# Scan inputs: log(1+e) on one vector engine at full width, magnitudes from the accumulator bank, delta ahead of C

## The reference, cut to what matters

```
xn = _rmsnorm(x, norm_w)
xz = xn @ W_in.T
xm, z = jnp.split(xz, 2, axis=-1)
...  (depthwise convolution over time, 4 taps)
xc = jax.nn.silu(xc + conv_b[None, :, None])
u = jnp.swapaxes(xc, 1, 2)
x_dbl = u @ W_x.T
dt, Bm, Cm = jnp.split(x_dbl, [DT_RANK, DT_RANK + D_STATE], axis=-1)
delta = jax.nn.softplus(dt @ W_dt.T + b_dt)
A = -jnp.exp(A_log)
y = _selective_scan(u, delta, A, Bm, Cm, Dp)
y = y * jax.nn.silu(z)
```

## Time and profile before

| | us |
|---|---|
| median of 3 runs | 3047.18 (3044.08 to 3047.55) |
| the profiled execution | 3044.58 |
| span of its trace | 3042.8 |
| TensorE busy | 2370.3 (78%) |
| VectorE busy | 1997.0 (66%) |
| ScalarE busy | 1772.5 (58%) |
| GpSimd busy | 1398.9 (46%) |
| block of `scan_inputs`, first sequence | 67.9 to 166.8 |
| block of `scan_inputs`, second sequence | 825.9 to 922.8 |

### The profile page before, as it was taken

How to read it: one execution, slowest core, us unless ns; L and a number is a source line. 1 busy time by engine, 2 the same in 40 slices (tenths; PEclk the granted TensorE clock), 3 DMA queues, 4 the chain that set the end, 5 groups by cost and what they waited for, 6 DMA issues and landing times. The chain is left out here.

```text
span 3042.8 us, 38732 instructions
## 1 busy us (share of the span) xinstructions
PE 2370.3 (78%) x12420; PEld 1202.1 (40%) x12421; DVE 1997.0 (66%) x1798; ACT 1772.5 (58%) x2733; POOL 1398.9 (46%) x540
## 2 busy tenths in 40 slices
PE   4678888888857888888886758797787499869668
PEld 1244444444324444444435123223222355545323
DVE  5689999999658999999965666515913222133440
ACT  3689999999478999999941430171064111122230
POOL 1489998999557999899941110000000300020000
PEclk7889999999988999999996878798889699979889
DMA  2130001000123000100000300010012300010000
GB/s 75 54 106 28 24 28 39 28 28 28 40 72 87 28 28 28 39 28 24 28 20 2 112 35 1 6 42 11 1 33 100 157 21 21 23 39 9 28 0 28
DMA packets 59819, 116.17 MB, mean 38 GB/s; under 512 B 13620, under 2 KB 21812, under 8 KB 58305
## 3 DMA queue, kind: packets, MB, share of 16 engines
q1 hardware_dynamic: 51104, 103.72, 10.6%
q0 software_dynamic: 8608, 11.05, 1.2%
HBM read 86.92 MB, written 27.53 MB: 38 GB/s over the span
## 5 line engine op out<-in xcount | busy, mean ns | idle before, releaser
L825 POOL TENSOR_TENSOR hs<-hs,c_bc 128x2048 f32<-128x2048 f32 x256 | 1166.2, 4556 | 67.0 <-DVE hs L876 49.3
L876 DVE TENSOR_TENSOR_SCAN hs<-decays,carry,ps 128x512 f32<-128x512 f32 x512 | 621.7, 1270 | 9.1 <-PE ps L903 8.4
L876 DVE TENSOR_TENSOR_SCAN hs<-decays,ps 128x512 f32<-128x512 f32 x512 | 610.9, 1215 | 21.0 <-PE ps L903 8.3
L911 PE MATMUL ps<-hs,sel 128*64 128x512 f32 x2048 | 498.4, 608 | 15.5 <-POOL hs L825 15.2
L839 ACT ACTIVATE decays<-delta_near,A 128x512 f32<-128x512 f32 x512 | 363.4, 723 | 23.2 <-DVEq L853 22.7
L903 PE MATMUL ps<-ident,dbu_even 128*128 128x128 f32 x2048 | 295.1, 283 | 91.9 <-DVE hs L876 63.2
L903 PE MATMUL ps<-ident,dbu_odd 128*128 128x128 f32 x2048 | 293.3, 282 | 92.3 <-DVE hs L876 60.6
L839 ACT ACTIVATE decays<-delta_far,A 128x512 f32<-128x512 f32 x512 | 358.8, 714 | 11.0 <-DVE hs L876 10.9
L847 ACT ACTIVATE dbu_odd<-du_turned,b_turned 128x512 f32<-128x512 f32 x512 | 360.8, 718 | 0.0
L847 ACT ACTIVATE dbu_even<-du_turned,b_turned 128x512 f32<-128x512 f32 x496 | 349.8, 718 | 0.0
L903 PEld LDWEIGHTS ps<-ident,dbu_even 128*128 128x128 f32 x2048 | 220.0, 141 | 241.9 <-DVE hs L876 192.5
(11 more groups left out here) (265 smaller groups left out, 2759.1 us busy)
## 6 DMA issues: line engine op xcount, KB each, us to landing
c_bc<-c_rows SPq DMA_DIRECT2D x256, 128.0 KB, 2.8
o_rows<-osb SPq DMA_DIRECT2D x32, 256.0 KB
u_rows<-u SPq DMA_DIRECT2D x4, 1024.0 KB, 8.8
d_rows<-delta SPq DMA_DIRECT2D x4, 1024.0 KB, 4.2
delta_near<-d_rows SPq DMA_DIRECT2D x4, 1024.0 KB, 9.6
hs<-u_rows SPq DMA_DIRECT2D x4, 1024.0 KB, 6.6
delta_far<-d_rows SPq DMA_DIRECT2D x4, 1024.0 KB, 12.1
w_down<-in_expert_proj SPq DMA_DIRECT2D x1, 4096.0 KB, 36.5
```

The source lines that it names most:

```text
L825: pool.tensor_tensor(x, x, spread(c_bc[:, g, :], 4), ALU.mult).then_inc(weighed.sem, 1)
L876: dve.tensor_tensor_scan(hs[:, quad % RING, n, :], decays[:, s % RING, :], ps[:, DBU + s % RING, :], carry[:, at(i * GB, g), blk] if q els ...
L911: mm = pe.matmul(ps[lo:lo + DB, ACC + quad % 2 * 2 + j // 2, :], k.sel2[:, :], hs[:, quad % RING, j, :], start=False, stop=False, skip_gro ...
```

## The change

The tile `e_` moves into the memory of `du_turned`, which is free until the `du` tiles are taken; in the listings of the changed kernel e therefore carries that name. The absolute value (Abs) and the positive part (Relu) are each taken straight from the bank with the bias, tile by tile. The bank of a delta tile is only given back after its Relu. The polynomial runs on VectorE alone, 128x2048 each; GpSimd has no part in it. In the list of products `delta` goes ahead of `C`, and the second half's `z` goes behind everything but `du`. ScalarE's order and SyncE's order of stores change too.

```diff
-    e_ = xm[:, :, :].rearrange("p c n -> p (c n)")[:, 0:CPB * CI * W].rearrange("p (h c n) -> p h c n", h=CPB, c=CI)
+    e_ = du_t[:, :, :].rearrange("p (h c) n -> p h c n", h=CPB)
...
     order = [(kind, h, m) for kind, h, tiles in (("xm", 0, CI), ("xm", 1, CI), ("z", 0, CI), ("low", 0, 1),
-                                                 ("C", 0, 1), ("delta", 0, CI), ("B", 0, 1), ("z", 1, CI),
-                                                 ("low", 1, 1), ("C", 1, 1), ("delta", 1, CI), ("B", 1, 1),
-                                                 ("du", 0, QT), ("du", 1, QT)) for m in range(tiles)]
+                                                 ("delta", 0, CI), ("C", 0, 1), ("low", 1, 1),
+                                                 ("delta", 1, CI), ("C", 1, 1), ("B", 0, 1), ("B", 1, 1),
+                                                 ("z", 1, CI), ("du", 0, QT), ("du", 1, QT)) for m in range(tiles)]
...
+    def softplus(dve, h):
+        cols = slice(h * W, (h + 1) * W)
+        x, e = delta[:, :, cols], e_[:, h]
+        n = h * SOFT
         for f, (_, b) in enumerate(LOG1P_PAIRS):
             dve.wait_ge(squared.sem, squared.at(h * PAIRS + f + 1))
             if f:
-                dve.wait_ge(soft_dve.sem, soft_dve.at(n + f))
-            sq = square[:, (h * PAIRS + f) % ROOM, part, :]
-            dve.scalar_tensor_tensor(p, sq, b, p if f else e, ALU.add, ALU.mult).then_inc(soft_dve.sem, 1)
-        dve.wait_ge(soft_dve.sem, soft_dve.at(n + PAIRS))
-        dve.scalar_tensor_tensor(p, e, LOG1P_REAL, p, ALU.add, ALU.mult).then_inc(soft_dve.sem, 1)
-        dve.wait_ge(soft_dve.sem, soft_dve.at(n + PAIRS + 1))
-        dve.wait_ge(positive.sem, positive.at(h + 1))
-        dve.scalar_tensor_tensor(x, p, LOG1P_LEAD, x, ALU.mult, ALU.add).then_inc(soft_dve.sem, 1)
-        dve.wait_ge(soft_dve.sem, soft_dve.at(n + PAIRS + 2))
+                dve.wait_ge(soft.sem, soft.at(n + f))
+            dve.scalar_tensor_tensor(poly[:], square[:, (h * PAIRS + f) % ROOM], b, poly[:] if f else e,
+                                     ALU.add, ALU.mult).then_inc(soft.sem, 1)
+        dve.wait_ge(soft.sem, soft.at(n + PAIRS))
+        dve.scalar_tensor_tensor(poly[:], e, LOG1P_REAL, poly[:], ALU.add, ALU.mult).then_inc(soft.sem, 1)
+        dve.wait_ge(soft.sem, soft.at(n + PAIRS + 1))
+        dve.wait_ge(taken.sem, taken.at(take_no["delta", h, CI - 1]))
+        dve.scalar_tensor_tensor(x, poly[:], LOG1P_LEAD, x, ALU.mult, ALU.add).then_inc(soft.sem, 1)
+        dve.wait_ge(soft.sem, soft.at(n + PAIRS + 2))
         dve.wait_ge(u_stored.sem, u_stored.at(16 * (h + 1)))
-        dve.tensor_tensor(u[:, part, cols], x, u[:, part, cols], ALU.mult).then_inc(soft_dve.sem, 1)
-
-    def softplus_pool(pool, h):
...
+        dve.tensor_tensor(u[:, :, cols], x, u[:, :, cols], ALU.mult).then_inc(soft.sem, 1)
...
-            def take_delta(h):
+            def magnitude_of(h):
                 for m in range(CI):
-                    take("delta", h, m, delta[:, m, h * W:(h + 1) * W], ACT.Identity, bias=vec[:, m, DC + 1:DC + 2])
+                    act.wait_ge(summed.sem, summed.at(index["delta", h, m] + 1))
+                    act.activation(e_[:, h, m, :], bank(("delta", h, m)), ACT.Abs, bias=vec[:, m, DC + 1:DC + 2])\
+                       .then_inc(magnitude.sem, 1)
+
+            def positive_of(h):
+                for m in range(CI):
+                    take("delta", h, m, delta[:, m, h * W:(h + 1) * W], ACT.Relu, bias=vec[:, m, DC + 1:DC + 2])
...
-                x = delta[:, :, h * W:(h + 1) * W]
-                act.wait_ge(taken.sem, taken.at(take_no["delta", h, CI - 1]))
-                act.activation(e_[:, h], x, ACT.Abs).then_inc(magnitude.sem, 1)
-                act.wait_ge(magnitude.sem, magnitude.at(h + 1))
+                act.wait_ge(magnitude.sem, magnitude.at((h + 1) * CI))
                 act.activation(e_[:, h], e_[:, h], ACT.Exp, scale=-1.0).then_inc(e_ready.sem, 1)
-                act.activation(x, x, ACT.Relu).then_inc(positive.sem, 1)
                 act.wait_ge(e_ready.sem, e_ready.at(h + 1))
 
-            def squares(h):
-                for f in range(PAIRS):
+            def squares(h, which):
+                for f in which:
                     n = h * PAIRS + f
                     if n >= ROOM:
                         old_h, old_f = divmod(n - ROOM, PAIRS)
-                        act.wait_ge(soft_dve.sem, soft_dve.at(old_h * SOFT_DVE + old_f + 1))
-                        act.wait_ge(soft_pool.sem, soft_pool.at(old_h * SOFT_POOL + 2 * old_f + 4))
+                        act.wait_ge(soft.sem, soft.at(old_h * SOFT + old_f + 1))
...
-            take_delta(0)
+            magnitude_of(0)
+            silu_u(1)
+            exponential(0)
+            squares(0, range(ROOM))
+            positive_of(0)
+            take_low(1)
+            magnitude_of(1)
+            squares(0, range(ROOM, PAIRS))
+            exponential(1)
+            positive_of(1)
             take_b(0)
-            silu_u(1)
+            take_b(1)
+            squares(1, range(PAIRS))
             take_z(1)
-            exponential(0)
-            squares(0)
-            take_low(1)
-            take_delta(1)
-            take_b(1)
-            exponential(1)
-            squares(1)
             first_products()
...
-            for h in range(CPB):
-                softplus_pool(pool, h)
...
+            store_u(0)
+            sp.wait_ge(u_stored.sem, u_stored.at(16))
+            store_u(1)
+            store_c(0)
+            sp.wait_ge(c_stored.sem, c_stored.at(16))
+            store_delta(0)
+            sp.wait_ge(d_stored.sem, d_stored.at(16))
+            spread_delta(k, sp, b, 0, near, d_near)
+            store_c(1)
+            store_delta(1)
```

More of the change, by code:

```diff
@@ L461, in bank @@
         return ps[:, index[tile] % 8, :]
-    def softplus_dve(dve, h):
-        cols, part = slice(h * W, (h + 1) * W), slice(0, DVE_PART)
-        x, e, p = delta[:, part, cols], e_[:, h, part, :], poly[:, part, :]
-        n = h * SOFT_DVE
+    def softplus(dve, h):
+        cols = slice(h * W, (h + 1) * W)
+        x, e = delta[:, :, cols], e_[:, h]
+        n = h * SOFT
         for f, (_, b) in enumerate(LOG1P_PAIRS):
@@ L478, in softplus_dve @@
-        dve.scalar_tensor_tensor(x, p, LOG1P_LEAD, x, ALU.mult, ALU.add).then_inc(soft_dve.sem, 1)
-        dve.wait_ge(soft_dve.sem, soft_dve.at(n + PAIRS + 2))
-        dve.wait_ge(u_stored.sem, u_stored.at(16 * (h + 1)))
-        dve.tensor_tensor(u[:, part, cols], x, u[:, part, cols], ALU.mult).then_inc(soft_dve.sem, 1)
-    def softplus_pool(pool, h):
-        cols, part = slice(h * W, (h + 1) * W), slice(DVE_PART, CI)
-        x, e, p = delta[:, part, cols], e_[:, h, part, :], poly[:, part, :]
-        n = h * SOFT_POOL
-        def step(instruction):
-            nonlocal n
-            n += 1
-            instruction.then_inc(soft_pool.sem, 1)
-            pool.wait_ge(soft_pool.sem, soft_pool.at(n))
-        pool.wait_ge(e_ready.sem, e_ready.at(h + 1))
-        step(pool.tensor_scalar(p, e, LOG1P_LEAD, LOG1P_LEAD * LOG1P_REAL, ALU.mult, ALU.add))
-        step(pool.tensor_tensor(p, p, e, ALU.mult))
-        for f, (_, b) in enumerate(LOG1P_PAIRS):
-            sq = square[:, (h * PAIRS + f) % ROOM, part, :]
-            pool.wait_ge(squared.sem, squared.at(h * PAIRS + f + 1))
-            step(pool.tensor_scalar(sq, sq, 1.0, b, ALU.mult, ALU.add))
-            step(pool.tensor_tensor(p, p, sq, ALU.mult))
-        pool.wait_ge(positive.sem, positive.at(h + 1))
-        step(pool.tensor_tensor(x, x, p, ALU.add))
-        pool.wait_ge(u_stored.sem, u_stored.at(16 * (h + 1)))
-        step(pool.tensor_tensor(u[:, part, cols], x, u[:, part, cols], ALU.mult))
@@ L654, in _ @@
                 take(("C", h, 0), whole[:, h * W:(h + 1) * W], rows=DS)
-                softplus_dve(dve, h)
+                softplus(dve, h)
             for t in range(QT):
@@ L678, in _, with store_u @@
             d_rows = k.d_rows[b].rearrange("(c p) t -> p c t", p=P)
-            for h in range(CPB):
+            def store_u(h):
                 cols = slice(h * W, (h + 1) * W)
@@ L682, in _, with store_c, store_delta @@
                 sp.dma_start(k.u_rows[b][:, :, cols], u[:, :, cols]).then_inc(u_stored.sem, 16)
+            def store_c(h):
+                cols = slice(h * W, (h + 1) * W)
                 sp.wait_ge(taken_dve.sem, taken_dve.at(take_no["C", h, 0]))
                 sp.dma_start(k.c_rows[b][:, cols], whole[:, cols]).then_inc(c_stored.sem, 16)
-                if h == 0:
-                    sp.wait_ge(u_ready.sem, u_ready.at(2 * CI))
-                sp.wait_ge(soft_dve.sem, soft_dve.at(h * SOFT_DVE + PAIRS + 2))
-                sp.wait_ge(soft_pool.sem, soft_pool.at(h * SOFT_POOL + 2 * PAIRS + 3))
+            def store_delta(h):
+                cols = slice(h * W, (h + 1) * W)
+                sp.wait_ge(soft.sem, soft.at(h * SOFT + PAIRS + 2))
```

(12 more changed lines are left out.)

10 lines of the change are left out of this document (4 added, 6 removed).

## The result

The changed kernel takes 3024.15 us (median of 5 runs, 3018.51 to 3027.96), the kernel before 3044.08 (5 runs, 3040.97 to 3047.55). The ratio is 0.993 with a 95% interval of 0.9915 to 0.9946: a gain of about 20 us, clear of zero. The profiled executions say the same: 3024.15 with a span of 3022.2 against 3044.58 with 3042.8. The forecast was 3021 and 25 us. The time is 3 us off and the gain 5, in part because the kernel before came out 3 us lower in five runs (3044.08) than in the three that the forecast started from (3047.18).

The account below looks back on a forecast made before the run. Each block before a scan was taken to end on GpSimd's last polynomial product. 13.3 + 14.2 - 2.4 = 25.1 us off gives 3019.5 from 3044.58 or 3022.1 from 3047.18; predicted 3021, range 3016 to 3027.

Parts of the forecast that it names:

- VectorE's full-width price: Polynomial before each scan: a 2048-column VectorE operation takes 2.29 us, 2.32 a step when dependent.
- the line through three widths: VectorE two-input operations: 512, 1024 and 1536 columns at 0.69, 1.22 and 1.76 us, extended to 2.29 for 2048.
- The rival that took 2.70 for VectorE's own pace: Polynomial: VectorE's slow rows are its own pace, 3.60 us a full-width operation; change 3.5 us slower, 3050; 6 in 100.
- The schedule of the first sequence: Block before the first scan: product with `u` done at 148.7 instead of 161.98, 13.3 us less.
- the wait before the fourth step: First half's polynomial: VectorE waits some 8.3 us, from 114.1 until ScalarE's fourth square at 122.4.
- the ramp of the second delta: From the end of the second `low` take to the start of the last delta take: 5.99 us, second sequence 5.24.
- The second sequence: Block before the second scan: ends at 903.8 instead of 918.03, 14.2 us less.
- The table loads: Two added per sequence: before the gates, hidden; before the scan's first decay, costing 1.1 and 1.28 us.
- Store of delta: Block's end waits for the second delta store, 7 us lost in each, 3035; 6 in 100.
- swallowed start: Scan's start: the DMA wait absorbs the late start, 3018.7, or 3015 with TensorE at full clock; 8 in 100.

Follow-up runs that it names:

- e3_wide: Kernel before with only the polynomial moved wholly to VectorE at 128x2048, all orders as before; 3031.35 us, ratio 0.9957.
- e4_split: Changed kernel with GpSimd doing the fourth channel tile again, 1536 columns on VectorE and 512 on GpSimd; 3039.61 us, ratio 0.9981.
- e5_square: Changed kernel with the first half's fourth square right behind the other three on ScalarE; 3015.91 us, ratio 0.9908.
- e7_memory: Changed kernel with delta copied out of the bank first, Abs and Relu at 128x2048 from memory; 3024.5 us, ratio 0.9936.
- e9_scan_fill: Changed kernel with filler products on TensorE at the start of the first half's scan, table load kept; 3022.26 us, ratio 0.992.
- e11_both: e8_tight with TensorE filler products before the last du tiles and at the scan's start; 3000.16 us, ratio 0.9848.
- e8_tight: Changed kernel with another ScalarE order and a closing one-column exponential that loads the table before the scan; 3003.79 us, ratio 0.9866.

## Why the prediction was right

Direction, range and mechanism held; the gain was 20 us where 25.1 was forecast, and the terms show where the 4.6 us between 25.1 and the 20.5 of the table lie.

- *VectorE's full-width price*, 2.29 and 2.32 a step by the line through three widths: 2.29 and 2.32 to 2.33 measured. The rival that took 2.70 for VectorE's own pace is dead; e3_wide and e4_split show the slow rows come and go with GpSimd.
- *The schedule of the first sequence.* First delta magnitude forecast at 96.3, measured 96.27; squares' end 110.9 and 111.0; VectorE's start 107.2 and 107.27; the wait before the fourth step 8.3 and 8.91; end of `u` 148.7 and 149.49. The 0.8 us lie in one term, the ramp of the second delta: 5.99 assumed, 6.85 measured. Block gain 13.3 forecast, 12.5 measured.
- *The second sequence.* Here I took 5.24 for that ramp from the old trace, as if it belonged to the sequence. It was 6.58 (858.46 to 865.04). This is the weakest step of the block sum: 14.2 forecast, 13.0 measured. The ramp goes with TensorE's granted clock (0.72 with 5.24, 0.55 with 6.85, 0.57 with 6.58), and that differs between traces of the same code. So a ramp can't be priced from one row to better than 1.6 us, and that this term was off by only 0.9 and 1.3 was in part luck.
- *The table loads.* The first was hidden, as said (ScalarE done at 147.6, idle 6.80 before the scan). The second, 1.1 and 1.28, measured 1.33 and 3.65 in the scans' lengths, and 1.7 and 2.5 by the fourth quad. This term was mis-sized, by 2.6 us in this pair of traces and by 2 to 2.4 in the mean of all (two loads 4.4 us by the quads, 4.8 by the scans). I priced ScalarE's delay and not what an idle TensorE does with it. The bounds of 0 and 1.28 did not hold the value, since the upper one was the load alone. The Trainium skill's figure of 2.66 us for a switch ("ScalarE: Activation LUTs", What ACT_TABLE_LOAD costs) is nearer to these 2.2 to 2.4 a load, but for another reason: the decay starts 0.01 us behind the load's end (155.64, 155.65), so there is no drain to be seen.
- *Store of delta, swallowed start.* Neither happened. The delta store left at 147.19, and VectorE's takes ended the block.

What stays open: the scans' own scatter. With a load the two scans together take 1303.4 to 1307.7 us in seven kernels, without one 1299.1 to 1303.6 in six. A single scan says less than the sum: the second takes 639.9 to 640.8 us in four kernels that have the load (e4_split, e5_square, e7_memory, e9_scan_fill), which is under the 641.57 of the kernel before. So the 3.65 us of the second scan are not the load's alone. Within a group it isn't the fourth quad alone that sets the scans, and I haven't traced the rest.

## What to carry to other kernels

When two engines take turns on something, the work that is moved to one of them costs less than its width says; price it with rows that stand alone. A second engine on the same chain should be asked for what it costs the first. And when an engine is made late, ask what the engines behind it do meanwhile: here a TensorE left idle came back at a lower clock, a few filler products kept it at 1.00, and a table load put into ScalarE's idle time gave the scans their length back.

## What the runs showed of the hardware that I had not expected

- VectorE at 128x1536 with two inputs from memory takes 1.76 us when it starts with GpSimd idle and 2.04 to 2.72 when it starts beside one of GpSimd's operations. GpSimd's 128x512 product goes from 1.26 to 2.64 us or more. Both lose: three fourths of the work on one and a fourth on the other took 6 to 7 us longer in each sequence than all on one (e3_wide, e4_split).
- A ScalarE table load of 1.28 us at a scan's start puts the fourth quad 2.2 us later (mean of twelve starts 25.7 against 23.5 of eight), and 0.6 and 1.3 us when TensorE is kept busy with and without it (e9_scan_fill, e11_both).
- Sixteen transpositions behind 14.92 us of idle time (after) took 3.64 us at a granted clock of 0.50. Behind 6.8 us (e8_tight) they took 3.38 and 3.65 us at 0.56 and 0.50. Behind 5.3 us of filler work and 1.51 us of idle time it was 1.97 us at 1.00. A clock of 0.50 is the level of 1.2 GHz, 1.00 that of 2.4.
